# Head products of two f16 halves, and the next sequence's gate products before the last projection

## What is computed

```python
x = x + attn(layernorm(x))      # q, k: width 256; v, o: width 512; i, f: 8 gates each, capped at 15 by tanh
    # per head, over the tokens:
    m_new = max(log_sigmoid(f) + m, i);  F = exp(log_sigmoid(f) + m - m_new);  I = exp(i - m_new)
    C = F * C + I * k v^T;  n = F * n + I * k
    h = (q * scale) C / (max(|(q * scale) n|, exp(-m_new)) + 1e-6)
    # per head: minus mean, over standard deviation, times gamma; times sigmoid(o); times Wout^T
x = x + gelu(layernorm(x) @ ternary(w1)^T + b1) @ ternary(w2)^T + b2
```

## Time and profile before

| | us |
|---|---|
| median of 3 runs | 1876.2 (1874.89 to 1881.56) |
| the profiled execution's own time | 1875.94 |
| its span, first to last instruction | 1874.2 |
| PE busy | 1811.6 (97%) |
| PE weight loads busy | 945.5 (50%) |
| DVE busy | 1178.1 (63%) |
| ACT busy | 1034.3 (55%) |
| POOL busy | 507.4 (27%) |

### The profile page before, as it was taken

The page is one execution under the profiler, slowest core; times in us unless marked ns, Lnnn a source line. Parts: engine busy times, 40 slices in busy tenths (PEclk is TensorE's granted clock), DMA queues, the critical chain, the costliest instruction groups (busy, mean ns, idle before and its releaser), DMA issues.

```text
span 1874.2 us, 30222 instructions
## 1 busy us (share of the span) xinstructions
PE 1811.6 (97%) x11900; PEld 945.5 (50%) x11900; DVE 1178.1 (63%) x2259; ACT 1034.3 (55%) x1711; POOL 507.4 (27%) x394
## 2 busy tenths in 40 slices
PE   5769999999999999999999999999999999999989
PEld 3454554545455454545545454554545445454544
DVE  6686575665757566575765657576565756645542
ACT  5757647274563727456372745737274473736523
POOL 1342131412314141231413123141312214131220
PEclk8879999999999999999999999999999999999989
DMA  8434125240422515042251503225150332413010
GB/s 278 145 102 119 29 61 129 51 139 24 129 39 52 139 46 144 23 117 51 52 138 46 145 23 106 62 51 139 46 144 17 103 72 51 117 45 99 12 40 23
DMA packets 233517, 156.86 MB, mean 84 GB/s; under 512 B 195088, under 2 KB 199312, under 8 KB 228256
## 3 DMA queue, kind: packets, MB, share of 16 engines
q1 hardware_dynamic: 231792, 151.79, 30.8%
q10 hardware_dynamic: 1584, 3.15, 0.5%
HBM read 90.48 MB, written 17.24 MB: 57 GB/s over the span
## 4 chain that ended last, share of the span: by engine, by line
PE 92%; DVE 2%; ACT 1%; issue 1%; DMA 0%; POOL 0%; POOLq 0%; DVEq 0%; ACTq 0%
PE pf L1714 24%; PE pf L1728 24%; PE pa L1606 19%; PE pa L1582 8%; PE psh L1606 6%; PE psh L1687 5%; PE psh L1681 1%; PE psh L1665 1%; PE pa L1573 1%; PE psh L1647 1%; PE psh L1620 1%; ACT dec L842 0%; DVE x2T L1078 0%; DVE dec L1245 0%; DVE x2T L1090 0%
## 5 line engine op out<-in xcount | busy, mean ns | idle before, releaser
L1728 PE MATMUL pf<-w2T,gT 128*128 128x512 f16 x2048 | 535.8, 379 | 0.0
L1714 PE MATMUL pf<-x2T,w1T 128*128 128x512 f16 x2048 | 457.2, 381 | 0.8 <-DVE x2T L1322 0.6
L1330 DVE SCALAR_TENSOR_TENSOR gT<-g,wscale,gT 128x512 f16<-128x512 f32 x256 | 214.7, 839 | 287.2 <-ACT gT L865 287.2
L1728 PEld LDWEIGHTS pf<-w2T,gT 128*128 128x128 f16 x2048 | 223.9, 111 | 175.9
L1714 PEld LDWEIGHTS pf<-x2T,w1T 128*128 128x128 f16 x2048 | 194.1, 98 | 234.3 <-issue 2.5
L862 ACT ACTIVATE g<-pf,b1c 128x512 f32<-128x512 f32 x256 | 175.6, 686 | 100.9 <-PE pf L1714 88.5
L1606 PE MATMUL pa<-wT,xT 128*128 128x512 f16 x960 | 213.6, 380 | 1.0 <-ACT sig L801 0.9
L870 ACT ACTIVATE ktok<-kT 128x512 f32<-128x512 f32 x64 | 40.3, 630 | 315.0 <-DVE kT L1268 315.0
L1687 PEld LDWEIGHTS psh<-vaug,dec 128*128 128x128 f32 x1024 | 183.0, 193 | 15.4 <-DVE cst L1234 1.2
L865 ACT ACTIVATE gT<-g,wscale 128x512 f16<-128x512 f32 x256 | 184.8, 722 | 8.4
L574 POOL TENSOR_TENSOR hinv<-hvar,half 128x8 f32<-128x8 f32 x64 | 105.0, 1640 | 298.4 <-DVE hvar L1281 298.4
(11 more groups left out here) (202 smaller groups left out, 2154.9 us busy)
## 6 DMA issues: line engine op xcount, KB each, us to landing
dec<-gate_r SPq DMA_DIRECT2D x32, 1024.0 KB, 6.5
xin<-L_attn_x SPq DMA_DIRECT2D x16, 1024.0 KB, 5.3
out<-x1b SPq DMA_DIRECT2D x64, 256.0 KB, 2.2
xres<-L_attn_x SPq DMA_DIRECT2D x16, 512.0 KB, 6.3
xres<-L_attn_x SPq DMA_DIRECT2D x32, 256.0 KB, 2.9
qw<-gate_w SPq DMA_DIRECT2D x128, 48.0 KB, 5.8
gT<-L_ffn_w SPq DMA_DIRECT2D x5, 1024.0 KB, 5.0
gT<-L_ffn_w ACTq DMA_DIRECT2D x3, 1024.0 KB, 6.3
```

Source lines behind the costliest of these rows:

```text
L1330: nc.vector.scalar_tensor_tensor(gT[:, LO, f, :], g32[:, f % 2, :], wscale[:, W_GELU:W_GELU + 1], gT[:, HI, f, :], ALU.mult, ALU.subtract) ...
L1714: last = nc.tensor.matmul(bank, w1T[:, k, tok(f)], x2T[:, part, :, k, :], start=(k == 0 and part == HI), stop=(k == KD - 1 and part == LO))
L1728: last = nc.tensor.matmul(bank, gT[:, part, f, tok(t)], w2T[:, f, :], start=(f == 0 and part == HI), stop=(f == NF - 1 and part == LO), sk ...
```

## The change

1. Head products of sequences 1 to 15: `dec` and `vaug` are each split into f16 halves. ACT writes the high half of `dec` (`decay_hi`), DVE (chunks 0, 1) or POOL (chunks 2, 3) the rest (`decay_lo`); POOL writes the high half of the values (`value_hi`), DVE the rest (`value_lo`). A head has two products of 130 columns: high and low half of `dec`, each with both halves of the values side by side. Chunk 0's halves lie in `qT`, those of chunk j in the f32 columns of `dec` of chunk j-1, so each split waits for the one before. The value halves share space with `hoT` (`shared`).
2. `head_stats` begins with the sum of the two value columns from PSUM into an SBUF tile (`head_sum`, in `ktok`), which frees the bank; norms, head sums and centring read that tile. Sequence 0 copies instead. Scales are folded in elsewhere (`head_scale`, `V_SPLIT`, `SCORE_SPLIT`).
3. `gates(b + 1)` on PE stands before `project(b, 3)`, which takes the other bank of `pa`; `gate_sum` and `gate_minus` of b+1 stand on DVE before residual 3.
4. DVE's statistics of the x ahead: tiles 0, 1 behind `head_stats` 3, tiles 2, 3 between residual 0 and 1. ACT's `tokens_hi(b + 1)` stands behind `gate_columns`.

The core of the diff:

```diff
         def pa_index(b, use):
...
+            if use == U_GATE and b > 0:
+                return at(b, PA_USES, 2 * KD - 1)
+            swapped = 1 if use == U_Y + T - 1 and b < B - 1 else 0
...
+            def value_hi(b, t):
+                pool.wait_ge(pa_fill, pa_filled(b, score_use(NH - 1)))
+                nc.gpsimd.tensor_copy(vparts[:, t, :, 0:VA], vaug[:, t, :, :]).then_inc(vhi_ok, 1)
+            def decay_lo(b, j):
+                pool.wait_ge(dec_hi_ok, at(b - 1, T, j + 1))
+                nc.gpsimd.tensor_tensor(dec_parts(j)[:, :, LO, :], dec[:, :, tok(j)], dec_parts(j)[:, :, HI, :],
+                                        ALU.subtract).then_inc(dec_lo_ok[j], 1)
...
                 for n in range(NH // 2):
                     earlier_only(b, n)
+                    if n in (1, 2) and not first:
+                        value_hi(b, 2 * n - 2)
+                        value_hi(b, 2 * n - 1)
+                if not first:
+                    decay_lo(b, 2)
                 head_norm(b, 0)
+                if not first:
+                    decay_lo(b, 3)
...
+            def decay_hi(b, j):
+                if j == 0:
+                    act.wait_ge(masked, at(b, NH // 2, NH // 2))
...
+                else:
+                    act.wait_ge(dec_lo_ok[j - 1], at(b - 1, 1, 1))
+                nc.scalar.activation(dec_parts(j)[:, :, HI, :], dec[:, :, tok(j)], ACT.Copy).then_inc(dec_hi_ok, 1)
...
-                    for f in range(NF):
+                    for f in range(NF - 3):
                         gelu(fb, f)
+                    decay_hi(b, 0)
+                    for f in range(NF - 3, NF):
+                        gelu(fb, f)
+                    decay_hi(b, 1)
...
+                if run_f:
+                    decay_hi(b, 2)
                 squares(b, 0)
                 if run_f:
                     sigmoids(b)
+                    decay_hi(b, 3)
...
-                nc.vector.tensor_tensor(den_of, norms, gtok[:, j, ROW_EM, :].rearrange("p (a h) -> p a h", h=H4), ALU.max)
+                if isinstance(b, int) and b == 0:
+                    nc.vector.tensor_copy(sum_by_group, by_bank[:, :, :, :, 0]).then_inc(ph_free, 1)
+                else:
+                    nc.vector.tensor_reduce(sum_by_group, by_bank, AX.X, ALU.add).then_inc(ph_free, 1)
+                dve.wait_ge(ph_free, at(b, PH_USES, U_H + j + 1))
+                nc.vector.scalar_tensor_tensor(den_of, gtok[:, j, ROW_EM, :].rearrange("p (a h) -> p a h", h=H4),
+                                               head_scale[:, 0:1], norms, ALU.mult, ALU.max)
...
+                    parts = dec_parts(j)
+                    nc.tensor.matmul(psh[:, i, 2 * g * VA:2 * (g + 1) * VA], parts[:, h, HI, :], vparts[:, j, h, :],
+                                     start=(j == 0 and g == 0), stop=False, skip_group_check=True)
+                    last = nc.tensor.matmul(psh[:, i, 2 * g * VA:2 * (g + 1) * VA], parts[:, h, LO, :], vparts[:, j, h, :],
+                                            start=False, stop=(g == HG - 1), skip_group_check=True)
...
-                project(b, 3)
                 if ahead:
                     x_ready(b + 1)
+                    gates(b + 1)
+                project(b, 3)
```

More of the change, by code:

```diff
@@ L254, in block_program @@
         kq_split = sem("kq_split")
+        vhi_ok, vlo_ok = sem("vhi_ok"), sem("vlo_ok")
+        dec_hi_ok = sem("dec_hi_ok")
+        dec_lo_ok = [sem(f"dec_lo_ok{j}") for j in range(T)]
+        cent_ok = sem("cent_ok")
         sq_ok = sem("sq_ok")
@@ L265, in pa_index, with pa_bank @@
         def pa_index(b, use):
-            if isinstance(b, int) and b == 0:
-                return KD + use + 2 * sum(use >= pair for pair in X_PAIRS)
-            return at(b, PA_USES, 2 * KD + use)
+            if use == U_GATE and b > 0:
+                return at(b, PA_USES, 2 * KD - 1)
+            swapped = 1 if use == U_Y + T - 1 and b < B - 1 else 0
+            if b == 0:
+                return KD + use + 2 * sum(use >= pair for pair in X_PAIRS) + swapped
+            return at(b, PA_USES, 2 * KD + use) + swapped
+        def pa_bank(b, use):
+            return pa_index(b, use) % 2
         def pa_filled(b, use):
@@ L275, in pa_taken @@
         def pa_taken(b, use):
-            if isinstance(b, int) and b == 0:
-                return pa_index(b, use) // 2
-            return at(b, PA_USES // 2, KD + use // 2)
+            return pa_index(b, use) // 2
         def pa_done(b, use):
@@ L794, in value @@
                 nc.scalar.activation(vaug[:, t, :, 0:DHV], bank.rearrange("p (h v) -> p h v", v=DHV),
-                                     ACT.Copy, scale=evac[:, W_V:W_V + 1]).then_inc(free, 1)
+                                     ACT.Copy, scale=V_SPLIT).then_inc(free, 1)
             def output_gate(b, *ns):
@@ L880, in sequence @@
                 run_f = fb is not None
-                if run_f and ahead:
-                    tokens_hi(b + 1)
                 gates(b, fb)
@@ L886, in sequence @@
                     gate_columns(b)
+                    if ahead:
+                        tokens_hi(b + 1)
                     queries(b, 0, 1)
@@ L1393, in sequence @@
                 state(b, 1)
-                hidden(10, 11, 12)
-                between(0)
-                state(b, 2)
-                hidden(13, 14, 15)
+                for t in range(T):
+                    if run_f:
+                        value_lo(b, t)
+                    hidden(10 + t)
+                    if t == 2:
+                        between(0)
+                        state(b, 2)
+                if run_f:
+                    decay_lo(b, 0)
+                    hidden(14, 15)
+                    decay_lo(b, 1)
                 def done(t):
@@ L1426, in sequence @@
                 done(2)
-                next_stats(*(range(3, T) if run_f else range(T)))
+                if run_f:
+                    next_stats(0, 1)
                 gated(b, 3)
@@ L1431, in sequence @@
                 residual(b, 0, ca)
+                next_stats(*(range(2, T) if run_f else range(T)))
                 between(6)
@@ L1438, in sequence @@
                 done(3)
+                if ahead:
+                    gate_sum(b + 1)
+                    gate_minus(b + 1)
                 residual(b, 3, ca)
@@ L1534, in take_pa @@
                 if not (isinstance(count, int) and count == 0):
-                    pe.wait_ge(pa_free[use % 2], count)
-                return pa[:, use % 2, :]
+                    pe.wait_ge(pa_free[pa_bank(b, use)], count)
+                return pa[:, pa_bank(b, use), :]
             def take_pf(fb, use):
@@ L1674, in chunk_state @@
                     pe.wait_ge(masked, at(b, NH // 2, NH // 2))
+                    if not (isinstance(b, int) and b == 0):
+                        pe.wait_ge(vlo_ok, at(b - 1, T, T))
+                if not (isinstance(b, int) and b == 0):
+                    pe.wait_ge(dec_lo_ok[j], at(b - 1, 1, 1))
                 if j == 1:
@@ L1686, in chunk_head @@
                 g, i = divmod(h, H4)
-                last = nc.tensor.matmul(psh[:, i, g * VA:(g + 1) * VA], dec[:, h, tok(j)], vaug[:, j, h, :],
-                                        start=(j == 0 and g == 0), stop=(g == HG - 1), skip_group_check=True)
+                if isinstance(b, int) and b == 0:
+                    last = nc.tensor.matmul(psh[:, i, 2 * g * VA:(2 * g + 1) * VA], dec[:, h, tok(j)], vaug[:, j, h, :],
+                                            start=(j == 0 and g == 0), stop=(g == HG - 1), skip_group_check=True)
+                else:
+                    parts = dec_parts(j)
[3 more added lines that the diff above has]
+                                            start=False, stop=(g == HG - 1), skip_group_check=True)
                 if h == NH - 1:
```

113 lines of the change are left out of this document (72 added, 41 removed).

## The result

| | us |
|---|---|
| median of 4 runs after the change | 1901.9 (1900.58 to 1903.43) |
| median of 4 runs before it, same chip | 1878.5 (1874.89 to 1881.56) |
| ratio, with its 95% interval | 1.0132 (1.0114 to 1.0149) |
| the profiled execution's own time after | 1901.34, span 1899.6 |

The change made the kernel 1.3% slower; I had forecast 0.6% slower, 1887 us: the right direction, and less than half of the size. 1901.9 lies 0.1 us inside the range (1853 to 1902), which left out most of the case that came.

The account below looks back on a forecast made before the run. The prediction took PE's instructions to bound the kernel, busy 109.80 of 109.85 us a sequence. From 1875.9 us it added 14.3 for sequences 1 to 13 and took off 3.0 for 14 and 15: 1887 us, range 1853 to 1902.

Parts of the forecast that it names:

- Head products: On PE, a head falls from 0.169 to 0.113 us, saving 1.8 us a sequence and 26.9 us over sequences 1 to 15.
- The slow pair: Rival: a head on PE costs 0.162 us, but the chain sets the period; 1890 us; chance 0.04.
- Added work: New copies and subtractions on ACT, DVE and POOL; POOL's subtraction 2.3 us, value halves under the GELU pairs cost nothing.
- the early stall: Rival: POOL's value copies at 1.7 us hold DVE's GELU halves, PE waits for ACT; up to 1901 us; chance 0.06.
- Who blocks whom: POOL's tensor passes hold up DVE's two-SBUF and scalar instructions, while POOL's power and DVE's PSUM reads pass.
- the chain: Through ACT, DVE and POOL, the gate product of chunk 3 comes at 1023.35 (before 1021.10); residual 2 reads its bank at 1032.3.
- The moved gates and the banks: The last projection waits for residual 2; PE stalls some 2.9 us in all, 1.1 us more a sequence after the saving.
- PE's clock: Rival: a 2.6 us stall in each sequence slows PE, 1.35 us more each, 17.5 in all; 1905 us; chance 0.10.
- Sequence 0 "keeps its f32 heads": Term of the sum: sequence 0 keeps its f32 heads, with no cost or saving entered for it.
- The sum: Whole kernel: +14.3 for sequences 1 to 13, -3.0 for 14 and 15, on 1875.9; 1887 us.
- The other side: Rival: the chain isn't the bound; POOL's subtraction at 1.1 us gives 1857 us, DVE never held 1853; chance 0.32.

Follow-up runs that it names:

- e5: Changed kernel with the subtractions decay_lo(2) and decay_lo(3) done by DVE behind the centring of chunks 0 and 1, not by POOL; 1871.6 us, ratio 0.9976.
- e1: Changed kernel with DVE's four scalings norm_apply(b + 2) moved from in front of residual 2 to behind gate_sum(b + 1); 1858.1 us, ratio 0.9890.
- e2: Changed kernel with PE computing the gate products of sequences 2 to 14 twice into the same bank; 1887.1 us, ratio 1.0048.
- e8: e7 with sequence 0 centred straight out of PSUM, without the copy of 128x520; 1854.4 us, ratio 0.9889.
- e9: e1 with sequence 0 centred straight out of PSUM, the statistics not moved; 1854.1 us, ratio 0.9880.
- e10: e9 with the two subtractions done by DVE as in e5; 1849.4 us, ratio 0.9851.
- e7: e1 with the statistics of tiles 2 and 3 of the x ahead and their small steps moved in front of gated(b, 3); 1862.0 us, ratio 0.9921.

## Why the prediction was right on the stall and wrong on the clock

- **Head products**: right. 0.056 us a head were forecast, 1.8 a sequence; the period without a wait is 1.87 shorter. The slow pair (0.162 us a head) fell with it: a 512-column product and a head take 0.33 us together.
- **Added work**: right. POOL's subtraction 2.13 (2.3 forecast), DVE's sum 1.24 (1.2). POOL's value copies take 0.83 us on average, not the 1.7 of the early stall, and PE has no wait under the GELUs.
- **Who blocks whom, the chain**: right, as e5 shows; DVE's second norm step of chunk 1 is held for 1.92 us, chunk 2 waits for `gated_lo(0)`. Too long at one link: chunk 2's bank was to be read 0.3 us after PE could use it, but the sum that frees it ends at 914.95 and PE's products of chunk 3 start at 915.17, so that stall did not occur.
- **The moved gates and the banks**: right in place and releaser, and close in size: 2.44 us against 2.6. Net of the saving that is 0.61 a sequence where 1.1 was forecast, and 13 of them made 7.9 us, not 14.3.
- **PE's clock: the failed step.** The prediction had the mechanism as a rival with a chance of 0.10 and put it at nothing in the sum; it measured 15.2 us. Its price was near, 1.35 us a stretch against 1.69. That the total came so close, 17.5 against 15.2, is luck: it took 13 stretches at too low a price, and nine came. The chance was too low. One row of the same trace showed the slow clock after an idle of 2.90 us, another place did after 2.16, and the forecast's own stall was 2.6; a stall of that size was the forecast, so its consequence belonged in the sum. e1 and e2 confirm the cause from two sides: with no idle time, or with less idle time under the same wait, there is no slow stretch.

  The place that I passed over, in the trace of the kernel before (PE's timeline of sequence 0): the f16 transposes behind the idle stand 0.11 us apart, where those of the earlier trace rows take 0.056.

```profile
147.95 0.27 PE L1526 MATMUL pf<-ident,x2T 128*128 128x128 f16 x1 [2.16 <-DVE x2T L1092]
148.01 0.31 PE L1527 MATMUL pf<-ident,x2T 128*128 128x128 f16 x1
148.12 0.31 PE L1528 MATMUL pf<-ident,x2T 128*128 128x128 f16 x1
```

- **Sequence 0 "keeps its f32 heads"**: the second term put at nothing, and wrong as a reason for it; up to sequence 1 it measured 6.4 us. The heads stay, but `head_stats` got a copy of 0.69 us per chunk, in the one sequence where PE waits for DVE. By e1, e8, e9 and e10 this and the scalings' place cost 3 to 4.6 us there, most of it again as a lower granted clock of PE; up to 3.9 us of the start can be chance.
- **The sum, term by term**: the stalls of sequences 1 to 13 7.9 where 14.3 was forecast, sequences 14 and 15 with the end -4.2 (-3.0), the clock 15.2 (0), sequence 0 6.4 (0). The first two would have made the forecast too high, and so hid a part of the other two.
- **The other side** (POOL's subtraction at 1.1 us, or DVE never held; 1857 and 1853): POOL's subtraction took 2.13 and DVE was held. That e9 took 1854 is no support for it: there DVE is held as before, and only the order differs.

Open: what decides that 9 of 13 equal waits were followed by the slow clock and four were not, and that in e7 a wait of 2.43 us was followed by none. The trace shows an order in it. Here are the 2.7 us from PE's restart in five sequences in a row after the change (windows view, columns as in the earlier trace rows; the granted clock is the third number from the end):

```profile
714.33:717.03 2.70, 2.70 (x8) 0.99 (x9) 1.93 (x3) 0.70 (x1) 1.20 (x1) 0.56 0.18 68
826.60:829.30 2.70, 2.70 (x8) 1.00 (x9) 1.92 (x3) 0.71 (x1) 1.20 (x1) 0.63 0.17 66
938.85:941.55 2.70, 2.70 (x9) 1.07 (x10) 1.92 (x3) 0.71 (x1) 1.21 (x1) 0.70 0.17 66
1051.09:1053.79 2.70, 2.70 (x13) 1.27 (x14) 1.93 (x3) 0.70 (x1) 1.21 (x1) 1.00 0.17 65
1161.66:1164.36 2.70, 2.70 (x7) 0.98 (x8) 1.92 (x3) 0.71 (x1) 1.20 (x1) 0.53 0.21 69
```

In all 13 the mean is 1.00, 0.66, 0.74, 1.00, 0.56, 0.63, 0.70, 1.00, 0.53, 0.60, 0.67, 0.74, 1.00. From one sequence to the next the clock falls about 0.4 us later after the restart, until one keeps the full clock, and then it begins again. So it isn't chance in each sequence but something that drifts evenly against the sequences.
The Trainium skill ("TensorE: Matmul & The Clock Gate", Part 1, "What's actually happening") says that the monitor behind the clock gate runs free of the kernel, so that the moment of a change varies. That would fit this drift; no run here moved the waits against it on purpose, so it stays argued.

## What to carry over

When a product is moved ahead of another and they share banks, look at what stands in front of the bank's reader on its own engine: here four scalings that nobody needed yet, at the end of a chain that came 3.4 us later than before, cost 13 waits, and moving that one call was worth 2.3% of the time. Price a forecast stall of PE together with the clock that may fall after it, as one term. And a change that saves on the bound engine by loading its suppliers needs their slack counted link by link, also in the sequence that "stays as it is".
